# Mixture-of-experts layer: dense experts replaced by sorted rows, indirect transfers and a last summing pass

## Chip, cores, metric

One core of a Trainium2 chip runs the whole program. The metric is the device time of one launch in microseconds (us), median of several runs.

## What is computed

The input is `x`, 8 batches of 2048 rows of 256 numbers (16384 rows). First comes a landmark attention with 16 heads of 16 and 64 landmarks, with a residual and a layer norm; then a top-2 mixture of 8 experts, again with residual and layer norm:

```
x = layernorm(x + attention(x))
gate_logits = x @ Wg.T + bg                      # 8 experts
vals, idx   = top_k(gate_logits, 2)
gate_w      = softmax(vals)
all_out     = einsum('nd,ehd->neh', x, We) + be  # every expert, 256 x 256
out         = sum(all_out[idx] * gate_w)         # the two chosen ones
x = layernorm(x + out)
```

The kernel works in 32-bit floats. A product of full precision is made of three TensorE products with each factor split into a high and a low part (`product3`: high x high, low x high, high x low).

## The kernel before

A program for each engine is written out by hand; engines wait on semaphores, and instructions of one engine run in the order written. All plain transfers are issued by SyncE (SP), in one queue. The rows are cut into 32 chunks (`NCH`) of 512 (`CH`), four tiles (`TPC`) of 128 rows each.

Stage one (up to about 602 us) projects keys and values of all chunks, makes the landmark sums and inverts the landmark kernels. It is not touched, apart from the load of the experts' bias.

Stage two does, for each chunk: project queries (`queries`: TensorE L1618, ScalarE L805, VectorE `queries_lo` L1199); stack them by head with 16 transfers into the one buffer `q_stack` (`stack_queries_hi`, `stack_queries_lo`, `stack_query_norms`, L431 to L451); distances of eight head pairs (`query_dists`) and their exponentials into the one buffer `phi` (`q_exps`, L829) with a clamp on VectorE; `denominators` (L1663), their reciprocal, stored to memory and spread back over `attn` by two transfers (`store_inverses`, `spread_inverses`, L454, L462); `attention` and its scaling (`normalise`); split of the result (`attn_hi` on ScalarE L841, `attn_lo` on GpSimd L599); `output_projection` (L1688); `residual_stats` (VectorE L1254), `ln1` (GpSimd L615), `normalise_rows` (ScalarE L855); transposes of the rows, gate logits, their transpose, and the gates (`gates_begin`, `gates_end`).

Experts: `experts(p, n)` (L1749), 16 calls a chunk, each six products of 512 columns, so two experts for one tile of 128 rows; all eight experts are computed for every row. The results are weighed with the gate (zero for an expert not chosen): half of them on VectorE (`combine`, L1331), half on ScalarE (`weigh`, L891), whose parts GpSimd sums (`sum_parts`, L621). `finish`, `ln2` and `result` do the second layer norm, and the chunk is stored.

The loop `for p in range(NCH)` stands once in each engine's program (SP L528, GpSimd L641, ScalarE L941, VectorE L1393, TensorE L1794). In iteration p the experts work on chunk p, the first layer norm on c = p + 1, and the attention on q = p + 2 and q + 1. Two extracts give the order on ScalarE and TensorE: ScalarE runs `q_exps(q, 4..8)` with `weigh` between them, then `queries(q + 1)`, then `normalise_rows(c)`; TensorE runs `query_dists(q, 6..8)`, `experts`, `queries(q + 1)`, `denominators(q)`, and the 16 expert calls lie between all other steps.

Of the kernel before, what the change touches and what calls it, by code (L numbers as in the profile page):

```python
# [37 lines left out]
SLOTS = 32  # L38
PIVOTS = (3, 3, 3, 3, 3, 4, 4, 4, 4)


C_ID, C_HEAD, C_NEG, C_LO, C_M16, C_NSEL, C_IOTA, C_EXP, C_BES, C_EPS, C_MINUS, C_REG, C_END = (
    0, 128, 136, 200, 201, 217, 225, 233, 237, 238, 242, 246, 278)


def program(nc, xT, x, wq, wk, wv, wo, we, wg, bq, bk, bv, bo, be3, bg, temp, idx, gbase, consts, tri, out):
# [10 lines left out]
    xT_v = xT.rearrange("(k p) t -> p k t", p=P)  # L57
    x_v = x.rearrange("(c t p) d -> c p t d", t=TPC, p=P)
    out_v = out.rearrange("(c t p) d -> c p t d", t=TPC, p=P)

    ctx = ExitStack()
    with ctx:
# [3 lines left out]
        def sem(name):  # L66
            return ctx.enter_context(nc.semaphore(name))

# [36 lines left out]
        be_s = sb("be_s", [P, 2 * D], f32r)  # L105
# [11 lines left out]
        part_x = sb("part_x", [P, 2, KC, 2 * D])  # L117
# [4 lines left out]
        with nc.sbuf_tensor("augk0", [64, CH], f32r) as augk0, nc.sbuf_tensor("aug_hi", [32, CH], f32r) as aug_hi:  # L122
            augk = [augk0]
        y_spare = sb("y_spare", [P, TPC, D])
# [10 lines left out]
        st2, mv2, ve2, rs2, nm2 = (sb("st2", [P, TPC, 6]), sb("mv2", [P, TPC, 2]), sb("ve2", [P, TPC]),  # L135
                                   sb("rs2", [P, TPC]), sb("nm2", [P, TPC]))
        nt1, nt2 = sb("nt1", [P, TPC]), sb("nt2", [P, TPC])
        lg, m8, i8 = (sb("lg", [P, TPC, E]), sb("m8", [P, TPC, 8]),
                           sb("i8", [P, TPC, 8], u32))
        if2, gd, ge, gs, gw1, gw2 = (sb("if2", [P, TPC, 2]), sb("gd", [P, TPC]), sb("ge", [P, TPC]),  # L140
                                     sb("gs", [P, TPC]), sb("gw1", [P, TPC]), sb("gw2", [P, TPC]))
        oh1, oh2, gate, gate_h = (sb("oh1", [P, TPC, E]), sb("oh2", [P, TPC, E]),
                                  [sb(f"gate{i}", [P, TPC, E]) for i in range(2)],
                                  sb("gate_h", [P, TPC, E], f32r))
        g_st, g_t = sb("g_st", [P, TPC, 32]), sb("g_t", [P, P], f32r)
        logit_rows = sb("logit_rows", [P, P])


        with ExitStack() as stage1:
# [9 lines left out]
            with ExitStack() as setup:  # L159
                def sb0(name, shape, dt=f32):  # L160
                    return setup.enter_context(nc.sbuf_tensor(name, shape, dt))

                bdh = [sb0(f"bdh{i}", [P, KC, HPS, NL], f32r) for i in range(2)]
                bdl = [sb0(f"bdl{i}", [P, KC, HPS, NL], f32r) for i in range(2)]
                augm = [sb0(f"augm{i}", [64, KC, HPS, NL], f32r) for i in range(2)]
                be_raw, be_tmp = sb0("be_raw", [P, 2 * D]), sb0("be_tmp", [P, 2 * D], f32r)
# [5 lines left out]
        x_tok, y_out = sb("x_tok", [P, TPC, D]), [sb("y_out", [P, TPC, D]), y_spare]  # L172
        x1 = [sb(f"x1_{i}", [P, TPC, D]) for i in range(2)]
        x1h, x1l = [sb("x1h0", [P, KC, CH], f32r)], [sb("x1l0", [P, KC, CH], f32r)]
        x1h.append(sb("x1h1", [P, KC, CH], f32r))
        x1l.append(sb("x1l1", [P, KC, CH], f32r))
        parts = [[part_x[:, i, k] for k in range(KC)] for i in range(2)]
# [8 lines left out]
        we_raw = [a[:].rearrange("p t d -> p (t d)") for a in (*x1, *y_out)]  # L186
# [37 lines left out]
        wo_done, h_done, ln1_stats, ln1_coef, x1_ready, x1t_done, x1h_ready, x1l_ready = (  # L224
            sem("wo_done"), sem("h_done"), sem("ln1_stats"), sem("ln1_coef"), sem("x1_ready"),
            sem("x1t_done"), sem("x1h_ready"), sem("x1l_ready"))
        logits_done, logits_saved, gate_done, gate_read, gd_ready, ge_ready, gst_ready, gtr_done, gt_ready, be_done, be_added = (
            sem("logits_done"), sem("logits_saved"), sem("gate_done"), sem("gate_read"), sem("gd_ready"), sem("ge_ready"), sem("gst_ready"),
            sem("gtr_done"), sem("gt_ready"), sem("be_done"), sem("be_added"))
        ffn_done, comb_done, part_ready, part_sum, acc_done, ln2_stats, ln2_coef, res_ready, res_stored = (  # L230
            sem("ffn_done"), sem("comb_done"), sem("part_ready"), sem("part_sum"), sem("acc_done"), sem("ln2_stats"), sem("ln2_coef"),
            sem("res_ready"), [[sem(f"res_stored{i}{half}") for half in range(2)] for i in range(2)])
# [5 lines left out]

        def raw(ap):

            return ap.bitcast(f32)
# [37 lines left out]
        def expert_bank(p, n):  # L279

            return bank[(2, 3, 5)[(16 * p + n) % 3]]
# [26 lines left out]
        def _(sp):  # L308
# [3 lines left out]
            sp.sem_inc(acc_done, 2)  # L312
# [8 lines left out]
            for dst, src in ((cst, consts), (bq_sb, bq), (bk_sb, bk), (bv_sb, bv), (bo_sb, bo), (bg_sb, bg),  # L321
                             (temp_sb, temp), (be_raw, be3)):
# [163 lines left out]
            def store(p, half):  # L486

                sp.wait_ge(res_ready, TPC * p + 2 * half + 2)
                sp.dma_start(out_v[p, :, 2 * half:2 * half + 2],
                             y_out[p % 2][:, 2 * half:2 * half + 2]).then_inc(res_stored[p % 2][half], 16)  # L490
# [8 lines left out]
            for i in range(2 * KC):  # L499
# [1397 lines left out]
```

## Time and profile before

| | us |
|---|---|
| median of 3 runs | 2072.36 (2070.72 to 2078.35) |
| the profiled execution | 2077.58 |
| its span, first to last instruction | 2075.8 |

The busy time of each engine (us, share of the span, instructions), and the span in 40 equal slices, each digit the busy share in tenths; PEclk is TensorE's granted clock in tenths of full speed, DMA the mean busy share of the 16 DMA engines:

```profile
PE 1795.9 (87%) x18232; PEld 1363.1 (66%) x18232; DVE 1358.9 (65%) x3414; ACT 1141.1 (55%) x2171; POOL 753.2 (36%) x1113
...
PE   4578999999965699999989999899999899998987
...
PEclk9689999999986799999999999999999999999999
DMA  2686797778862444444553344443445434445310
```

PE is TensorE's products, PEld its weight loads, DVE VectorE, ACT ScalarE, POOL GpSimd, SPq the transfers that SP issues. A timeline row is start, length, engine, line, operation, output<-input and count; in brackets the idle time of the engine before it and what ended it. Products overlap: the distance between two starts says more than one's length.

### The profile page before, as it was taken

Reading aid. Unit: us, or ns where it says so; the run is one execution under the profiler, and the core shown is the slowest. Engines: PE = TensorE matmul, PEld = TensorE weight load, DVE = VectorE, ACT = ScalarE, POOL = GpSimd, SP = SyncE. Lnnn points to the kernel's source line nnn. Section 1 sums busy time; section 2 is a strip of 40 time slices with the busy share of each in tenths; the row PEclk is TensorE's granted clock in tenths of the full one; section 3 lists DMA queues with packets and bytes.
Section 4 is the critical chain, followed back from the end, with each engine's and each line's share of the span. In section 5 each row is a group of like instructions: output and inputs, shape, how many; then the busy total and the mean of one; then the engine's idle time right before and its main releaser. Section 6 shows DMA issues by size and latency. Waiting matters only on the chain. (4 is left out here: it accounts for less than half of the span.)

```text
span 2075.8 us, 46584 instructions
## 1 busy us (share of the span) xinstructions
PE 1795.9 (87%) x18232; PEld 1363.1 (66%) x18232; DVE 1358.9 (65%) x3414; ACT 1141.1 (55%) x2171; POOL 753.2 (36%) x1113
## 2 busy tenths in 40 slices
PE   4578999999965699999989999899999899998987
PEld 3167778778753466666666666666666666666666
DVE  5678845987334466776666766677766667666765
ACT  2256666667554365556556555555655654664533
POOL 2300000000002245555455554555555545545544
PEclk9689999999986799999999999999999999999999
DMA  2686797778862444444553344443445434445310
GB/s 84 97 169 145 168 189 169 166 164 185 162 184 73 90 109 107 93 92 92 114 114 87 88 99 109 110 102 89 93 98 116 107 83 93 93 108 112 77 38 26
DMA packets 223805, 233.38 MB, mean 112 GB/s; under 512 B 59873, under 2 KB 147297, under 8 KB 223329
## 3 DMA queue, kind: packets, MB, share of 16 engines
q1 hardware_dynamic: 223392, 229.87, 50.0%
q8 instruction: 144, 2.36, 0.5%
q14 instruction: 77, 0.62, 0.1%
q0 software_dynamic: 192, 0.52, 0.1%
HBM read 78.28 MB, written 25.69 MB: 50 GB/s over the span
## 5 line engine op out<-in xcount | busy, mean ns | idle before, releaser
L302 PE MATMUL bank<-weh,x1h 128*128 128x512 f32 x1024 | 441.5, 431 | 0.0
L304 PE MATMUL bank<-wel,x1h 128*128 128x512 f32 x1024 | 413.0, 403 | 0.0
L303 PE MATMUL bank<-weh,x1l 128*128 128x512 f32 x1024 | 412.4, 403 | 0.0
L897 ACT ACTIVATE part_x<-bank,gate 128x256 f32<-128x256 f32 x512 | 214.7, 471 | 285.9 <-PE bank L304 285.7
L838 ACT ACTIVATE phi<-bank,nlt,invt 128x512 f32<-128x512 f32 x256 | 185.2, 778 | 167.6 <-PE bank L1643 167.6
L302 PEld LDWEIGHTS bank<-weh,x1h 128*128 128x128 f32 x1024 | 199.5, 195 | 116.6 <-issue 77.1
L612 POOL TENSOR_TENSOR x_tok<-x_tok,bo_sb 128x512 f32<-128x512 f32 x64 | 81.5, 1299 | 529.7 <-DMA x_tok<-in_x 529.7
L625 POOL TENSOR_TENSOR part_x<-part_x 128x512 f32<-128x512 f32 x128 | 165.0, 1289 | 289.4 <-ACT part_x L897 289.4
L304 PEld LDWEIGHTS bank<-wel,x1h 128*128 128x128 f32 x1024 | 197.5, 193 | 48.1
L303 PEld LDWEIGHTS bank<-weh,x1l 128*128 128x128 f32 x1024 | 198.3, 194 | 35.3
L700 ACT ACTIVATE phi<-bank,invt 128x512 f32<-128x512 f32 x256 | 162.6, 684 | 106.6 <-PE bank L1532 106.3
L1531 PE MATMUL bank<-l_hh,k_hl 128*128 128x256 f32 x512 | 146.3, 317 | 39.8 <-DMA k_hl<-kh 29.0
L1068 DVE TENSOR_SCALAR phi<-phi,phi_max,phi_min 128x1024 f32<-128x1024 f32 x128 | 103.7, 810 | 106.0 <-ACT phi L700 105.8
L1252 DVE TENSOR_TENSOR attn<-bank,attn 128x512 f32<-128x512 f32 x64 | 43.8, 688 | 157.5 <-DMA attn<-den_dram 157.4
L1220 DVE TENSOR_SCALAR phi<-phi,phi_max,phi_min 128x1024 f32<-128x1024 f32 x128 | 131.2, 1026 | 17.0 <-ACT phi L838 16.8
L586 POOL TENSOR_TENSOR ve<-mv,cst 128x1 f32<-128x1 f32 (+1 forms) x160 | 46.2, 289 | 258.3 <-DVE mv L1355 157.9
L1531 PEld LDWEIGHTS bank<-l_hh,k_hl 128*128 128x128 f32 x512 | 100.6, 197 | 55.7 <-DMA k_hl<-kh 34.5
L1684 PE MATMUL bank<-phi,y_cur 128*32 128x512 f32 x512 | 72.1, 637 | 71.1 <-DVE attn L1252 71.1
L1532 PE MATMUL bank<-l_lo,k_ha 128*128 128x256 f32 x512 | 132.3, 289 | 0.0
L1643 PE MATMUL bank<-q_stack,l_stack 128*128 128x512 f32 x256 | 92.8, 445 | 45.6 <-DMA q_stack<-key_aug 34.8
L603 POOL TENSOR_TENSOR attn_l<-attn,attn_h 128x512 fp32r<-128x512 f32 x64 | 84.6, 1324 | 114.1 <-ACT attn_h L846 114.1
L302 PE MATMUL bank<-xh,wh 128*128 128x512 f32 x260 | 108.5, 417 | 13.3 <-DVE xl L1088 6.9
(200 smaller groups left out, 4111.1 us busy)
## 6 DMA issues: line engine op xcount, KB each, us to landing
x_raw<-in_xT SPq DMA_DIRECT2D x64, 512.0 KB, 5.1
q_stack<-kh SPq DMA_DIRECT2D x256, 128.0 KB, 2.4
x_tok<-in_x SPq DMA_DIRECT2D x32, 512.0 KB, 3.8
q_stack<-kl SPq DMA_DIRECT2D x128, 128.0 KB, 2.7
q_stack<-key_aug SPq DMA_DIRECT2D x128, 128.0 KB, 5.5
attn<-den_dram SPq DMA_DIRECT2D x64, 256.0 KB
k_hl<-attn_h SPq DMA_DIRECT2D x32, 256.0 KB, 4.7
k_ha<-attn_h SPq DMA_DIRECT2D x32, 256.0 KB, 5.1
```

The costliest lines, as they stand in the source:

```text
L302: nc.tensor.matmul(outp, ah, bh, start=first, stop=False)
L303: nc.tensor.matmul(outp, al, bh, start=False, stop=False)
L304: return nc.tensor.matmul(outp, ah, bl, start=False, stop=last)
L625: own.then(nc.gpsimd.tensor_tensor(a[0], a[0], a[1], ALU.add))
L700: nc.scalar.activation(phi[:, n], bank[6 + s][:], ACT.Exp, scale=invt[:]).then_inc(exp_done, 1)
L838: nc.scalar.activation(phi[:, i], bank[6 + i % 2][:], ACT.Exp, bias=nlt[:, c // CPB, i:i + 1], scale=invt[:]).then_inc(qexp_done, 1)
L897: last = nc.scalar.activation(parts[t % 2][n % 4 // 2][:, u * D:(u + 1) * D], expert_bank(p, n)[:, u * D:(u + 1) * D], ACT.Copy, scale=gat ...
L1068: V.tensor_scalar(tile, tile, phi_max[:], phi_min[:], ALU.min, ALU.max).then_inc(phi_ready, 1)
L1220: V.tensor_scalar(two, two, phi_max[:], phi_min[:], ALU.min, ALU.max).then_inc(qphi_ready, 2)
L1531: mm(dst, k_hl[at][:, g, tok], wide(hh), start=True, stop=False)
L1532: last = mm(dst, k_ha[at][:, g, tok], wide(lo), start=False, stop=True)
L1643: mm(bank[6 + i % 2][:], l_stack[c // CPB % 2][:, i].rearrange("p u k -> p (u k)"), q_stack[:, i], start=True, stop=True).then_inc(qdist_d ...
```

## The change

The experts leave the loop. After the gates of chunk p, VectorE finds each row's place in the region of its two experts (`find_places`, with ranks that TensorE counts by products in `ranks`), and GpSimd writes the chunk's rows there by eight indirect transfers of 128 rows of 260 numbers: the row, the two gates, its number, its first expert (`scatter`). Every fourth chunk VectorE plans which tiles of which expert are full (`plan`). After the loop there are 264 tiles of 128 rows: SP loads a tile from an address in a register, TensorE transposes it, ScalarE and VectorE split it, TensorE multiplies it with the expert whose number it loads into registers and adds the bias; ScalarE or VectorE weighs; GpSimd writes the terms back to each row's place by two indirect transfers for two tiles. The residual is part of the first expert's term (the identity is added to the weights). Then a last pass loads both terms of each chunk, adds, normalises and stores. The expert weights are loaded and split in iterations 1 to 5 of the loop and no longer ahead of it. The orders within an iteration change too.

```diff
+ROW = D + 4
+QUAD = 4
+ROWS_OF = (3, 7, 11, 15, 19, 23, 27, 31)
+TAKEN = (24, 32, 32, 32, 32, 32, 32, 32, 16)
+TILES = sum(TAKEN)
+IN_RING, OUT_RING, SUM_RING = 3, 4, 4
 ...
+            def load_tiles(n):
 ...
+                _, at = nc.values_load_multi_w_load_instructions(
+                    tile_row[0:1, QUAD * n:QUAD * (n + 1)], [mybir.EngineType.SP], ...)
+                for i in range(QUAD):
+                    sp.dma_start(tile_in[:, QUAD * ring + i], rows_dram[bass.ds(at[i], P), :]).then_inc(tile_loaded[ring], 16)
+            def load_terms(c):
+                ring = c % SUM_RING
+                if c >= SUM_RING:
+                    sp.wait_ge(res_stored[ring], 16 * (c // SUM_RING))
+                for u, dst in enumerate((term_a, term_b)):
+                    sp.dma_start(dst[ring], terms_v[u, c]).then_inc(sum_loaded[ring], 16)
+            def store(c):
+                sp.wait_ge(res_ready, TPC * (c + 1))
+                sp.dma_start(out_v[c], term_a[c % SUM_RING]).then_inc(res_stored[c % SUM_RING], 16)
 ...
@@ SP: the loop and what follows
-                if p:
-                    store(p - 1, 0)
                 load_rows(q)
+                store_inverses(q)
                 stack_queries_hi(q + 1)
-                store_inverses(q)
                 stack_queries_lo(q + 1)
                 spread_inverses(q)
                 stack_query_norms(q + 1)
-                if p:
-                    store(p - 1, 1)
                 load_query_x(q + 3)
+                load_weights(p)
+            for n in range(TILES // QUAD):
+                load_tiles(n)
+            for i in range(OUT_RING):
+                sp.wait_ge(term_stored[i], 32 * len(range(i, TILES // 2, OUT_RING)))
+            for c in range(SUM_RING):
+                load_terms(c)
+            for c in range(NCH):
+                store(c)
+                if c + SUM_RING < NCH:
+                    load_terms(c + SUM_RING)
@@ GpSimd: the loop and what follows
                 ln1(c)
-                sum_parts(p, 0)
                 residual(q)
-                ln2(p, 0)
-                sum_parts(p, 1)
+                scatter(p)
                 split_lo(q + 2, 1)
                 attn_lo(q, 0)
-                ln2(p, 1)
-                sum_parts(p, 2)
                 attn_lo(q, 1)
+            scatter_pads()
+            for m in range(TILES // 2):
+                scatter_terms(m)
+            for c in range(NCH):
+                ln2(c)
@@ ScalarE: the loop, as it is after
+                q_exps(q, range(4, 6))
+                x1_copy(p)
+                q_exps(q, range(6, 8))
+                normalise_rows(c, c % 2)
+                save_logits(p)
+                queries(q + 1)
+                gate_exp(p)
+                query_hi(q + 2, 1)
+                if begins_batch(q + 1):
+                    for g in (1, 2):
+                        landmarks_of_batch((q + 1) // CPB, g)
+                q_exps(q + 1, range(0, 2))
+                attn_hi(q, 0)
+                attn_hi(q, 1)
+                if begins_batch(q + 2):
+                    landmarks_of_batch((q + 2) // CPB, 0)
+                q_exps(q + 1, range(2, 4))
+                weights_hi(p)
@@ VectorE: the loop, as it is after
+                q_clamp(q, range(4, 6))
+                residual_stats(c, c % 2)
+                q_clamp(q, range(6, 8))
+                gates_begin(p)
+                invert_denominators(q)
+                queries_lo(q + 1)
+                gates_end(p)
+                find_places(p)
+                query_norms(q + 1)
+                normalise(q, 0)
+                normalise(q, 1)
+                weights_lo(p)
+                q_clamp(q + 1, range(0, 4))
+                if p in ROWS_OF:
+                    plan(ROWS_OF.index(p))
@@ TensorE: the loop and what follows, as they are after
+                x1_transposes(p)
+                query_dists(q, range(4, 6))
+                output_projection(c)
+                gate_logits(p)
+                query_dists(q, range(6, 8))
+                logit_transpose(p)
+                denominators(q)
+                queries(q + 1, 1)
+                attention(q, 0)
+                ranks(p)
+                query_norms(q + 1)
+                attention(q, 1)
+                query_dists(q + 1, range(0, 4))
+                if begins_batch(q + 1):
+                    z_transposes((q + 1) // CPB)
+                    landmark_solve((q + 1) // CPB)
+            tile_transposes(0)
+            for m in range(TILES // 2):
+                if m % 2 == 0:
+                    numbers = experts_of_quad(m // 2)
+                if m + 1 < TILES // 2:
+                    tile_transposes(m + 1)
+                expert(m, numbers)
```

`expert(m, ...)` does two tiles, each six products of 256 columns and one for the bias. `scatter(p)` waits for `find_places(p)`, and `residual_stats(c)` for the scatters of chunk c - 2.

## Rows read from the trace of the kernel before

**Rows 1.** Stretches: length, engines' busy us (count), granted clock, DMA share, GB/s

```profile
602.00:624.00 22.00, 6.37 (x65) 4.67 (x65) 3.95 (x8) 12.05 (x31) 2.52 (x2) 0.69 0.87 227
684.00:700.00 16.00, 0.74 (x9) 0.50 (x2) 1.83 (x4) 1.51 (x3) 2.51 (x2) 0.55 1.01 173
1100.00:1200.00 100.00, 92.81 (x675) 69.22 (x677) 70.81 (x204) 57.61 (x117) 53.61 (x83) 0.98 0.40 92
```

**Rows 2.** Costliest group of the page: operation, count, busy us and mean ns, idle before

```profile
L302 PE MATMUL bank<-weh,x1h 128*128 128x512 f32 x1024 | 441.5, 431 | 0.0
```

**Rows 3.** Timeline of the transfer queue and ScalarE: start us, us, operation

```profile
680.90 5.97 SPq L428 DMA_DIRECT2D q_stack<-kh  x8
...
1946.73 5.10 SPq L428 DMA_DIRECT2D q_stack<-kh  x8
1990.44 0.60 SPq L460 DMA_DIRECT2D den_dram<-den_inv  x1
...
2002.17 0.63 ACT L846 ACTIVATE attn_h<-attn 128x512 fp32r<-128x512 f32 x1 [2.84 <-DVE attn L1252]
```

**Rows 4.** Timeline of the fill, each link of a chunk's chain on its engine

```profile
623.95 1.22 PE L1643 MATMUL bank<-q_stack,l_stack 128*128 128x512 f32 x2 [12.98 <-DMA q_stack<-key_aug]
624.79 1.45 ACT L838 ACTIVATE phi<-bank,nlt,invt 128x512 f32<-128x512 f32 x2 [6.38 <-PE bank L1643]
...
662.37 0.58 PE L302 MATMUL bank<-wh,attn_h 128*128 128x256 f32 x1 [1.69 <-POOL attn_l L603]
...
667.90 0.76 DVE L1261 TENSOR_TENSOR x<-bank,x_tok 128x256 f32<-128x256 f32 x2 [1.07 <-PE bank L304]
...
672.09 3.55 PE L1672 MATMUL bank<-phi,y_cur 128*32 128x128 f32 x64 [4.23 <-DVE phi L1220]
673.55 2.08 ACT L860 ACTIVATE x<-x,nm,rs 128x256 f32<-128x256 f32 x4 [12.06 <-POOL nm L589]
675.58 0.50 PE L302 MATMUL bank<-xh,wh 128*128 128x512 f32 x1
...
679.26 0.68 ACT L814 ACTIVATE sq<-bank,bq_sb 128x512 f32<-128x512 f32 x1
...
688.22 1.23 ACT L846 ACTIVATE attn_h<-attn 128x512 fp32r<-128x512 f32 x2 [3.70 <-DVE attn L1252]
688.93 2.51 POOL L603 TENSOR_TENSOR attn_l<-attn,attn_h 128x512 fp32r<-128x512 f32 x2 [5.46 <-ACT attn_h L846]
...
699.43 0.80 PE L1643 MATMUL bank<-q_stack,l_stack 128*128 128x512 f32 x1 [15.26 <-DMA q_stack<-key_aug]
```

**Rows 5.** Timeline of TensorE in the loop, at the full clock

```profile
1281.08 0.39 PE L302 MATMUL bank<-weh,x1h 128*128 128x512 f32 x1
1281.31 0.39 PE L303 MATMUL bank<-weh,x1l 128*128 128x512 f32 x1
...
1294.92 1.03 PE L1712 MATMUL bank<-cst,x 128*128 128x128 f32 x8
...
1322.96 0.28 PE L303 MATMUL bank<-wh,attn_l 128*128 128x256 f32 x1
1323.08 0.29 PE L304 MATMUL bank<-wl,attn_h 128*128 128x256 f32 x1
...
1331.85 1.95 PE L1672 MATMUL bank<-phi,y_cur 128*32 128x128 f32 x64
```

**Rows 6.** Timeline of GpSimd's indirect gathers, and their time to landing

```profile
5.52 0.95 POOL L559 DMA_INDIRECT phi<-in_x,rows_sb  x1 [0.30 <-issue]
6.78 0.95 POOL L559 DMA_INDIRECT phi<-in_x,rows_sb  x1 [0.31 <-issue]
...
DMA to landing us min/median/max: 3.8/4.8/6.7
```

**Rows 7.** Transfers by line: count, KB each, median us to landing

```profile
out<-y_out SPq DMA_DIRECT2D x32, 256.0 KB, 3.0
idx_sb<-in_idx SPq DMA_DIRECT2D x1, 0.5 KB, 1.9
```

More of the change, by code:

```diff
@@ L134, in program @@
                                    sb("rs1", [P, TPC]), sb("nm1", [P, TPC]))
[L135 to L146, printed above, removed]
+        nt1 = sb("nt1", [P, TPC])
         with ExitStack() as stage1:
@@ L227, in program @@
[L227 to L232, printed above, removed]
+            sem("x1t_done"), sem("x1c_ready"))
@@ L277, in begins_batch, with tile_batch @@
             return c % CPB == 0 and not past_end(c)
-        def expert_bank(p, n):
-            return bank[(2, 3, 5)[(16 * p + n) % 3]]
+        def tile_batch(n):
+            return next(s for s in range(len(TAKEN)) if n < sum(TAKEN[:s + 1]))
         def pairs_of(a, j, u=slice(None)):
@@ L1424, in _ @@
                     landmark_values((q + 1) // CPB)
-            finish(NCH - 1, 3)
+            pads()
+            plan(len(ROWS_OF))
+            pick(0)
+            tile_lo(0)
+            for m in range(TILES // 2):
+                if m % 2 == 0 and m // 2 + 1 < TILES // QUAD:
+                    pick(m // 2 + 1)
+                if m + 1 < TILES // 2:
+                    tile_lo(m + 1)
+                if m % 2 == 0:
+                    weigh(m)
+            for c in range(NCH):
+                sum_terms(c)
@@ L1720, in gate_logits @@
                 for k in range(KC):
[L1721 to L1724 removed]
+                    for t in range(TPC):
+                        last = mm(bank[2][32 * t:32 * t + 32, 0:P], wg_s[:, k], x1_T[:, k, t * P:(t + 1) * P],
+                                  start=(k == 0), stop=(k == KC - 1))
@@ new lines, in experts_of_quad, with expert @@
+            def experts_of_quad(n):
+                return nc.values_load_multi_w_load_instructions(
+                    tile_ei[0:1, QUAD * n:QUAD * (n + 1)], [mybir.EngineType.PE], min_val=0, max_val=E - 1,
+                    skip_runtime_bounds_check_because="an expert's number is a position among the eight")[1]
+            def expert(m, numbers):
+                pe.wait_ge(xt_l_ready, m + 1)
+                if m >= 2:
+                    pe.wait_ge(term_ready[m % 2], m // 2)
+                for i in range(2):
+                    dst, cols = bank[m % 2][:, i * D:(i + 1) * D], bass.ds(numbers[2 * (m % 2) + i] * D, D)
+                    for k in range(KC):
+                        at = slice((2 * i + k) * P, (2 * i + k + 1) * P)
+                        product3(dst, xt_h[m % 2][:, at], xt_l[m % 2][:, at], weh[:, k, cols], wel[:, k, cols], k == 0, False)
+                    last = mm(dst, ones32[:], be_s[:, cols], start=False, stop=True)
```

644 lines of the change are left out of this document (348 added, 296 removed).

## The prediction

> **What bounds the kernel now.** I read the stretches of the run first. TensorE is busy 93% of a hundred microseconds in the second stage at a granted clock of 0.98, while the DMA engines are at 0.40 [rows 1]; the costliest group is the experts' product with all eight experts, 1024 instructions for each of its three factors [rows 2]. A 512-column product starts 0.234 us after the one before, a 256-column one 0.12 us [rows 5]; so a chunk's 96 expert products hold TensorE 22.4 us. The loop over chunks is timed by the start of a chunk's first query-stacking transfer: 680.90 for chunk 2, 1946.73 for chunk 31, 29 chunks, 43.65 us each [rows 3]. The run is then stage one (to 602), a fill of some 100 us, 29 periods (1266 us), and an end of 110. The fill is where to look next: there the experts don't run yet, and each step of a chunk stands bare in time [rows 4].
>
> **What the change does to that.** It takes the expert products out of the loop and puts two serial phases behind it: 264 tiles through their expert, then a pass that loads both terms of each row, adds, normalises and stores. Expert work falls from 3072 products of 512 columns (3072 x 0.234 = 719 us) to 264 x 7 of 256 (1848 x 0.12 = 222 us). The gain can only come from a shorter loop period, so that is the first thing to work out.
>
> **The loop.** The instructions per chunk that stay are well below the period: TensorE 43.65 - 22.4 at most. What decides is the order. In the new ScalarE order `normalise_rows(c)` and `save_logits(p)` stand ahead of `queries(q+1)`, and on TensorE `logit_transpose(p)` and `denominators(q)` stand ahead of `queries(q+1)`. Before, the queries stood ahead of all of these. `output_projection(c)` needs `attn_hi(c)`, which now stands behind `q_exps(q, 0:2)`, and these need the queries of q stacked. So from "chunk q stacked" to "chunk q+1 stacked" there is one chain, and it is the period. Its links, each as the fill shows it [rows 4]: products and exponentials of two pairs, 623.95 to 626.24, 2.3; attention rows split high and low, 688.22 to 691.44, 3.2; output projection, 662.37 to 667.90, 5.5; residual, statistics and POOL's coefficients, 667.90 to 673.55, 5.65; normalising four tiles, 2.1; saving and transposing the logits, 0.6 (an estimate from a 128 x 128 copy's and a transpose's size); denominators, 3.55; queries from the first product to the last square, 675.58 to 679.94, 4.4; stacking, from the first transfer's issue to the first product that uses it, 680.90 to 699.43, 18.5 [rows 3, 4]. Sum 45.8: no link can start before the last one ends.
>
> Two bounds on it. The output projection and the denominators ran at the half clock in the fill, after the idle wait for stacking; at full clock they take 24 x 0.12 = 2.9 and 1.95 [rows 5], and the chain is 41.6. The granted clock was 0.55 while TensorE waited for the stacking and 0.69 in the stretch of 602 to 624 [rows 1]; the new loop has the same wait each chunk, so I take the half clock. Upwards: eight scatters of 128 rows a chunk (1.06 MB) run beside the stacking, because `find_places(p)` ends some 4 us after the queries. The DMA share was 1.01 at 173 GB/s there already [rows 1]; at the 227 GB/s of share 0.87 that is 1.06/0.261 = 4.1 us more at worst, and nothing at best, as the fill's stacking had 0.75 MB of other loads (query rows, inverse) issued behind it within the same stretch. I take nothing, and 4 for the range. Once in four chunks the landmark copies (2.8 us), the landmark solve (about 3) and the plan of tiles (some 20 small VectorE steps, 7 us, of which 4 stay uncovered by the output projection) fall into the chain: (2.8 + 3 + 4)/4 = 2.4. The period is then 45.8 + 2.4 = 48.2; I use 48, bounds 41.6 and 52. What stays hidden: POOL's eight scatter issues at 1.25 us each [rows 6], 10 us between the places and the next `attn_lo`, with about 3 us to spare (at 1.6 us each they would end too late); VectorE's gate work, beside ScalarE's queries and the stacking.
>
> **The start and the end of the loop.** Stage one is unchanged. In the fill the expert weights' load and split are gone; the residual there waited for the projection anyway, so only the stretched low split and some DMA time return, 3 us: chunk 2 is stacked at 699.4 - 3 = 696. Chunk 31 is stacked at 696 + 29 x 48 = 2088. From there: the chain up to the denominators once more, 2.3 + 3.2 + 5.5 + 5.65 + 2.1 + 0.6 + 3.55 = 22.9; reciprocal 1.3; store and spread of the inverses to the split, 1990.44 to 2002.17, 11.7 [rows 3]; split, projection, residual and normalising of chunk 31, 2.5 + 5.5 + 5.65 + 2.1 = 15.8; transposes, logits, gates and places about 8.5; the last plan 7. TensorE can begin on tiles 67 us after, at 2155. POOL issues chunk 31's eight scatters and eight of pads first: 60 + 20 = 80 us after.
>
> **The tile phase.** Per four tiles: TensorE 28 x 0.12 + 8 transposes in 1.03 [rows 5] = 4.4 us at full clock; POOL four scatters at 1.25 = 5.0 [rows 6]; DMA 1.06 MB, 4.1 us at the 261 GB/s above, 6.1 at 173. To these comes what no row shows: four loads of an expert's number into TensorE's registers, with TensorE waiting. Bounds: POOL's gap of 0.3 us between two issues [rows 6], where another engine hides it all, and the 1.9 us of the smallest transfer [rows 7] twice over. I take 1.4, nearer to the first, so 5.8 per four, 66 x 5.8 = 383 us; bounds 66 x 5.0 = 330 and, with a clock that stays at half (28 x 0.23 + 2 = 8.4, plus the loads), 66 x 9 = 594. One page has a price for the loads: the Trainium skill, DMA: Bandwidth & Descriptors, section Latency and other measured facts, gives about 600 ns as the floor of a tensor load. By an estimate from it, four in series would be 2.4 us, and the phase 66 x 6.8 = 449 us; no row here shows it. With 3 to fill the pipe and 5 for the last terms to land (indirect transfers landed in 3.8 to 6.7 us [rows 6]) the phase ends at 2155 + 391 = 2546.
>
> **The sum pass.** In SP's order `load_terms(c+4)` waits until the store of chunk c has landed, and `store(c+1)` is issued behind it. So each chunk costs the issue of two loads and a store, and the time of 1.57 MB to pass, in order, on one queue: at 261 GB/s 6.0, and about 1 of landing: 7.0 us; bounds 5 (a 256 KB store landed 3.0 after its issue [rows 7], and about 2 go to issuing) and 9 (at 173 GB/s). The engines are below that: residual, statistics and coefficients of such a chunk were 5.65 over two engines, normalising 2.1 [rows 4]. First store 13 us in, 28 x 7.0 = 196, four without loads 13, landing 4: 226 us. The same page's fit in Anatomy of one DMA (2.0 us and bytes over 436 GB/s) would by an estimate make 5.6 of a chunk, 40 us less in all; the highest rate that a stretch here shows is lower, and I go by that.
>
> **Sum.** 696 + 1392 + 67 + 391 + 226 = 2772 us of span; the profiled run took 2077.6 for a span of 2075.8, so 2774, **2775 us**. That profiled execution lies 5 us above the median of the three (2072.4), far below what is uncertain here. The kernel gets slower by a third: 497 us of TensorE's products go, but the loop was never 22 us from its next bound.
>
> **Rivals.**
> *The chain at full clock.* If TensorE keeps 2.4 GHz, period 41.6 and tiles at 5.0: 2775 - 29 x 6.4 - 53 = 2536. For it: the loop of before, with short gaps, held 0.98 [rows 1]. Against it: a wait of more than 10 us every chunk.
> *Tiles slower.* Register loads in series with a half clock, 9 us per four: 2775 + 211 = 2986. For it: it is the one price without a row.
> *The chain is shorter.* If stacking needs only its bytes at the highest rate (2.6 MB with the spread, at 261 GB/s 10 us, and 3 of landing), 5.5 us go from the chain: period 42.7, and 38.5 with the full clock too: 2620 or, with the tiles at 5.0 as well, 2447. For it: issue and landing could overlap better in a quiet queue. Against it: the one bare case took 18.5.
> *The other side: the loop falls to what the DMA engines need.* Per chunk 3.6 MB of today's 4.1 and 1.06 of scatters, 4.7 MB; at 227 GB/s 20.6 us, and if the chain runs over several chunks at once the period would be about 22: 2775 - 29 x 26 = 2021, faster by 3%. It decides below a period of (2077.6 - 696 - 67 - 391 - 226 - 1.8)/29 = 24.0 us. `q_stack`, `phi` and `attn` have one buffer each and the orders are fixed, which speaks against it.
> *It does not cut the work.* 264 tiles are always run, a quarter of the rows times experts and 3% more; I see no case in which it would run all.
>
> **Chances.** Forecast (2600 to 2950) 0.58; full clock 0.16; shorter chain 0.10; tiles slower 0.11; other side 0.03, a mixture near no change 0.02. A measurement of this kernel can tell about 0.5% from no change. Faster by over 0.5% 0.03, within 0.01, slower 0.96. The range takes in the full clock, half of the shorter chain and most of the slower tiles: 2450 to 2970.
>
> **What would show it.** In the changed kernel: stacking transfers 46 to 50 us apart in the loop, TensorE half idle with a granted clock well under 0.98; ScalarE's `kh` of the next chunk only after `x1` is normalised; a tile phase of 390 us with POOL and TensorE both near full; a last pass of 226 with the DMA engines as the only busy part. Wrong, if the stacking starts come under 40 us apart, if indirect issues take over 1.6 us each, or if SP does not wait for stores in the last pass.

## The result, and the profile after

The changed kernel takes 2849.16 us (median of 4 runs, 2844.34 to 2861.72) against 2071.54 (2069.52 to 2078.35) before: ratio 1.3755, 95% interval 1.3701 to 1.381. 2775 was forecast. The profiled execution has a span of 2847.8 us. Below, a time without a range comes from a single execution.

From the page of the changed kernel: engines' busy time, the 40 slices of TensorE, its granted clock and the DMA share, and the lines of the chain that ended last:

```profile
PE 1644.8 (58%) x17248; PEld 1247.9 (44%) x17248; DVE 1222.0 (43%) x3392; ACT 1045.6 (37%) x1891; POOL 901.1 (32%) x1001
...
PE   5589989974444454454544445445354699997000
...
PEclk8799999986666666566665666666666799999555
DMA  2868676844343433424334243342424366665666
...
DMA q_stack<-key_aug 8%; SPq L463 8%; PE bank L338 7%; DMA out<-phi 6%; PE bank L339 6%; PE bank L340 6%; PE bank L1826 4%; ACT phi L942 3%; PE bank L1921 2%; PE bank L1901 2%; SPq L486 2%; PE bank L1797 2%; PE bank L1685 2%; ACT x L964 2%; SPq L505 2%
```

Slices 10 to 30 are the loop: TensorE four to five tenths busy, at a clock of 0.6 where it held 0.98 [rows 1]. Then come five slices of tiles, TensorE full at full clock, and three of the sum pass, in which TensorE does nothing. The same in stretches (columns as in [rows 1]; loop, tiles, sum pass):

```profile
700.00:1500.00 800.00, 378.99 (x2931) 260.99 (x2929) 268.28 (x943) 251.01 (x467) 274.33 (x283) 0.64 0.38 100
2250.00:2550.00 300.00, 300.00 (x1916) 244.50 (x1915) 145.58 (x429) 101.92 (x212) 205.38 (x215) 1.00 0.61 189
2650.00:2810.00 160.00, 0.00 (x0) 0.00 (x0) 67.52 (x200) 47.68 (x92) 35.29 (x88) 0.50 0.70 222
```

The first stacking transfers of chunks 2 and 31 in the timeline of the queue, which give the period as [rows 3] did:

```profile
679.11 5.24 SPq L463 DMA_DIRECT2D q_stack<-kh  x8
...
2143.60 5.41 SPq L463 DMA_DIRECT2D q_stack<-kh  x8
```

29 periods of 50.50 us, against 43.65. So the parts of the span stand against the forecast like this (us):

| | forecast | trace |
|---|---|---|
| chunk 2 stacked (first product on it) | 696 | 696.6 |
| loop, chunk 2 stacked to chunk 31 stacked | 29 x 48 = 1392 | 2162.0 - 696.6 = 1465.4 |
| chunk 31 stacked to the first tile's transpose | 67 | 79.0 |
| tile phase, to the first load of the sum pass | 391 | 381.5 |
| sum pass | 226 | 225.3 |
| span | 2772 | 2847.8 |

The loop alone accounts for 73 of the 76 us missed, and the start of the tiles for 12; the tiles give back 10.

### The profile page after: what moved, and what is told of

Its sections match the earlier page's. It is cut to its first block, busy times and chain, and to the rows that moved or that the text cites. A ratio compares the mean times of both kernels' runs of the same rounds, so it can differ in the third digit from the quotient of the medians.

```text
span 2847.8 us, 46793 instructions
## 1 busy us (share of the span) xinstructions
PE 1644.8 (58%) x17248; PEld 1247.9 (44%) x17248; DVE 1222.0 (43%) x3392; ACT 1045.6 (37%) x1891; POOL 901.1 (32%) x1001
## 4 chain that ended last, share of the span: by engine, by line
PE 38%; DMA 17%; SPq 15%; DVE 10%; ACT 9%; issue 6%; POOL 5%; ACTq 0%; POOLq 0%; DVEq 0%
DMA q_stack<-key_aug 8%; SPq L463 8%; PE bank L338 7%; DMA out<-phi 6%; PE bank L339 6%; PE bank L340 6%; PE bank L1826 4%; ACT phi L942 3%; PE bank L1921 2%; PE bank L1901 2%; SPq L486 2%; PE bank L1797 2%; PE bank L1685 2%; ACT x L964 2%; SPq L505 2%
## 5 line engine op out<-in xcount | busy, mean ns | idle before, releaser
L711 POOL DMA_INDIRECT rows_dram<-x,place_i x256 | 248.3, 970 | 421.6 <-DVE place_i L1414 352.9
L1838 PE MATMUL bank<-phi,y_cur 128*32 128x512 f32 x512 | 93.8, 816 | 476.3 <-DVE attn L1349 476.3
L1349 DVE TENSOR_TENSOR attn<-bank,attn 128x512 f32<-128x512 f32 x64 | 44.1, 691 | 480.4 <-DMA attn<-den_dram 416.3
L1838 PEld LDWEIGHTS bank<-phi,y_cur 128*32 128x32 f32 x512 | 12.7, 123 | 495.4 <-issue 495.4
L1797 PE MATMUL bank<-q_stack,l_stack 128*128 128x512 f32 x256 | 150.2, 668 | 90.0 <-DMA q_stack<-key_aug 55.5
L338 PE MATMUL bank<-weh,q_stack 128*128 x528 | 174.5, 331 | 0.6 <-DVE q_stack L1485 0.6
L1485 DVE TENSOR_TENSOR q_stack<-bank,q_stack 128x512 fp32r<-128x512 f32 x132 | 91.3, 692 | 137.5 <-ACT q_stack L1008 137.5
L339 PE MATMUL bank<-weh,q_stack 128*128 x528 | 148.5, 281 | 0.0
L340 PE MATMUL bank<-wel,q_stack 128*128 x528 | 148.1, 280 | 0.0
L1797 PEld LDWEIGHTS bank<-q_stack,l_stack 128*128 128x128 f32 x256 | 62.0, 273 | 192.3 <-DMA q_stack<-key_aug 107.3
L730 POOL DMA_INDIRECT terms_dram<-attn,tile_to x132 | 126.6, 959 | 58.3 <-issue 20.4
L730 POOL DMA_INDIRECT terms_dram<-x_T,tile_to x132 | 126.6, 959 | 58.1 <-issue 20.4
L338 PE MATMUL bank<-wh,attn_h 128*128 128x256 f32 x256 | 97.6, 381 | 68.4 <-ACT x_T L974 66.3
L1008 ACT ACTIVATE q_stack<-bank 128x512 fp32r<-128x512 f32 x132 | 78.9, 598 | 157.1 <-PE bank L1901 157.1
```

Source lines behind the costliest of these rows:

```text
L338: nc.tensor.matmul(outp, ah, bh, start=first, stop=False)
L339: nc.tensor.matmul(outp, al, bh, start=False, stop=False)
L340: return nc.tensor.matmul(outp, ah, bl, start=False, stop=last)
L711: nc.gpsimd.indirect_dma_start(out=rows_dram, out_offset=bass.IndirectOffsetOnAxis(ap=place_i[:, at:at + 1].bitcast(u32), axis=0), in_=x1[ ...
L730: nc.gpsimd.indirect_dma_start(out=terms_dram, out_offset=bass.IndirectOffsetOnAxis(ap=tile_to[:, at:at + 1].bitcast(u32), axis=0), in_=te ...
L1797: mm(bank[6 + i % 2][:], l_stack[c // CPB % 2][:, i].rearrange("p u k -> p (u k)"), q_stack[:, i], start=True, stop=True).then_inc(qdist_d ...
```

## Experiments

Periods below are all read as above: the first stacking transfer of chunk 31 less that of chunk 2, over 29. "The change" is the changed kernel as it was measured above.

**The first look: the copy, and SyncE's wait in the sum pass.** TensorE's waits between 750 and 2000 us of the changed kernel (who waits, for whom: us in all, times, longest) hold one that my chain did not have, the last of these three:

```profile
PE bank L1838 <- DVE attn L1349: 387.9, 24, 18.8
PE bank L1797 <- DMA q_stack<-key_aug: 18.7, 22, 1.6
PE bank L338 <- ACT x_T L974: 55.5, 25, 3.5
```

L338 is the output projection, L974 is `x1_copy`. The first line says something else too: the long wait of each chunk, 16.2 us, ends for TensorE with the inverses of the denominators (L1838 is the second half of attention, L1349 its scaling), and behind that half TensorE waits another 0.85 us for the stacking (L1797 is the distances). Both go through SyncE's one queue, the spread of the inverses in the middle of the stacking, and they end nearly together. The waits of SyncE's queue in the sum pass (2640 to 2840 us):

```profile
SPq L565 <- DMA out<-phi: 152.5, 27, 6.1
```

```diff
-                q_exps(q, range(4, 6))
                 x1_copy(p)
+                q_exps(q, range(4, 6))
                 q_exps(q, range(6, 8))
@@ SP, sum pass
-                if c + SUM_RING < NCH:
-                    load_terms(c + SUM_RING)
+                if c and c - 1 + SUM_RING < NCH:
+                    load_terms(c - 1 + SUM_RING)
```

> Two edits, one in the loop and one in the sum pass, read apart in the trace. (a) ScalarE copies the first-layer rows of chunk p (x1_copy) ahead of q_exps(q, 4..6) and no longer behind. Theory, the copy is a missed link of the chain (output_projection waits for it through the bank that it frees, 2.2 us of TensorE's wait a chunk): the loop's period falls from 50.5 to about 48.4 us. Rival, the wait for the copy only covers another one that ends as late (the split rows of attention): the period stays within 0.5 us of 50.5. (b) In the sum pass SyncE issues the loads of a chunk one step later, so that the store they wait for has had a whole chunk's time to land. Theory, the pass is bound by the landing of the store just issued: 7.08 us per chunk falls to about 6.1. Rival, the DMA engines' rate is the bound: it stays at 7.0 or more. Both theories right: 2849 - 29 x 2.1 - 28 x 0.9 = about 2763 us in all.

2735.3 us. Period 48.22, 2.28 less. The wait is all but gone, in the same stretch:

```profile
PE bank L338 <- ACT x_T L974: 6.5, 9, 2.2
```

The sum pass takes 170.6 us in place of 225.3; its stores come 5.08 us apart (2582.74 to 2714.91, 26 steps), not the 6.1 expected, and the DMA engines are full, at a rate above all that the trace of before showed (2590 to 2640 us, columns as above):

```profile
2590.00:2640.00 50.00, 0.00 (x0) 0.00 (x0) 30.13 (x90) 20.74 (x40) 20.03 (x41) 0.50 0.97 314
```

So the wait for the store just issued was the bound (the DMA share was 0.70 with it), and the next one is the engines' rate, at 314 GB/s and not at 261.

**Queries first, and 128 rows in the bias product.**

```diff
@@ ScalarE
+                queries(q + 1)
                 normalise_rows(c, c % 2)
                 save_logits(p)
-                queries(q + 1)
@@ TensorE
-                logit_transpose(p)
+                queries(q + 1, 1)
                 denominators(q)
-                queries(q + 1, 1)
+                logit_transpose(p)
@@ VectorE: queries_lo, then invert_denominators, gates; SP: stack_queries_hi, then store_inverses
@@ buffers
-    be_s [32, E * D], ones32 [32, P]
+    be_s [P, E * D] (rows 32 to 127 zero), ones32 [P, P]
```

> Two edits, one in the loop and one in the tile phase. (a) The order of before for the queries: on all engines queries(q + 1) and the stacking of its high halves come ahead of the normalising, the logits and the denominators. Theory of the one chain: residual, statistics, coefficients, normalising, logits and denominators (5.65 + 2.1 + 0.6 + 3.1 us) leave the path from one stacking to the next as far as they are not needed, and the period falls from 50.5 to about 40 to 42 us. Rival, the stacking with its scatters and the inverses' way to memory and back is a chain of its own that ends as late: the period falls by less than 3 us. (b) The tiles' bias product takes 128 rows (96 of them zeros) and no longer 32. Theory, the change of the product's row count costs 0.3 to 0.4 us per tile: four tiles take 5.0 to 5.2 us (GpSimd's four indirect issues at 1.25 become the bound) instead of 5.62. Rival, the time behind the bias product is the wait for the next tile's split rows or the expert's registers: 5.6 stays. Both theories right: 2849 - 29 x 9 - 66 x 0.5 = about 2555 us; both rivals: above 2760.

2501.5 us; period 39.51, 11.0 less, a little more than expected: the one chain is borne out, and the order alone makes a fifth of the period. And the tiles come at 5.06 us per four, over all 264. Their timeline on TensorE, with 32 rows in the bias product (L1921) as the change has it,

```profile
2404.66 0.37 PE L338 MATMUL bank<-weh,q_stack 128*128 x1
...
2405.34 0.28 PE L340 MATMUL bank<-wel,q_stack 128*128 x1
2405.55 0.38 PE L1921 MATMUL bank<-be_s,ones 32*128 x1
2405.86 0.38 PE L338 MATMUL bank<-weh,q_stack 128*128 x1
```

and with 128:

```profile
2056.15 0.28 PE L338 MATMUL bank<-weh,q_stack 128*128 x1
...
2056.73 0.28 PE L340 MATMUL bank<-wel,q_stack 128*128 x1
2056.85 0.28 PE L1922 MATMUL bank<-be_s,ones 128*128 x1
2056.97 0.49 PE L1902 MATMUL bank<-cst,tile_in 128*128 128x128 f32 x3
```

Seven products take 1.20 us in the first and 0.82 in the second (0.92 for a tile that follows transposes, as the one shown in the first does). In the second GpSimd is next: its indirect issues lie 1.26 us apart, four of them 5.04.

**A busy TensorE for the clock, in two steps.** First 96 products that nobody reads, in the wait for the stacking:

```diff
                 query_norms(q + 1)
+                for _ in range(96): mm(bank[2][:, 256:512], wh.., wh.., start=True, stop=True)
                 attention(q, 1)
```

> In each iteration TensorE does 96 products of 256 columns whose result nobody reads, in its 15.6 us wait for the stacking. They cost no path time (11.5 us at full clock). Theory, the half clock that follows the wait costs the chain the difference between its rows at either level (output projection, denominators, attention: 5.5 to 2.9, 3.06 to 1.95, 1.94 to 1.06): granted clock in the loop from 0.64 to over 0.9, the period from 50.5 down to 46 to 47.5 us, the run to about 2740. Rival, the chain's links are bound by ScalarE and VectorE between the products, and the clock matters little: the period falls by less than 1.5 us though the clock rises. Second rival, the clock is granted by something other than recent work: it stays at 0.64 to 0.75.

2871 us, period 51.08: 0.6 more, where the theory expected 3 to 4.5 less. The test was not a fair one. The granted clock of the loop rose (0.77 of 700 to 2050 us, from 0.64), but not where the chain needs it. One iteration in stretches: the last of the dummies ends at 1464.2, and the chain goes on at 1468:

```profile
1458.00:1464.00 6.00, 6.00 (x52) 5.99 (x50) 0.00 (x0) 0.00 (x0) 4.62 (x5) 1.00 0.87 252
1464.00:1468.00 4.00, 0.30 (x6) 0.13 (x8) 0.69 (x1) 0.00 (x0) 2.66 (x3) 0.95 0.85 211
1468.00:1471.00 3.00, 1.83 (x8) 0.10 (x7) 0.69 (x1) 0.00 (x0) 0.00 (x0) 0.50 0.88 195
```

So the second step, dummies up to the end of this wait and of the one for the logits:

```diff
+                pe.wait_ge(qphi_ready, PAIRS * (q + 1))
+                for _ in range(24): mm(bank[7][:, 256:512], ...)
                 logit_transpose(p)
                 denominators(q)
 ...
-                for _ in range(96): ...
+                for _ in range(124): ...
                 attention(q, 1)
```

> The change as it is, with dummy products of 256 columns up to the end of both waits: 124 in the wait for the stacking (14.6 us of 15.6, up to about 1 us ahead of attention's second half) and 24 in the 6 us wait for the logits. In the run before, with 96, the granted clock was 1.00 during the dummies and 0.50 again 4 us after their end, so that the links of the chain still ran at the half clock. Theory, the chain pays for the half clock: now attention takes 1.06 and no longer 1.94, denominators 1.95 and no longer 3.1, the period falls by 2 to 3.5 us, to 47 to 48.5. Rival, the clock costs the chain little, since ScalarE and VectorE set the pace between the products: the period stays at 50 to 51 although these rows are at full clock.

2803.4 us, period 48.71: 1.8 less, with 0.87 in 700 to 2050. Now attention and denominators are rows of the full clock (1.06 and 1.95 us):

```profile
1823.65 1.06 PE L1838 MATMUL bank<-phi,y_cur 128*32 128x512 f32 x8 [1.88 <-DVE attn L1349]
...
1844.43 1.95 PE L1826 MATMUL bank<-phi,y_cur 128*32 128x128 f32 x64
```

But not the output projection. The denominators' products (L1826) and a third of the projection's (L339) between 750 and 2050 us, in the change and then here; behind the bar stand busy us and mean ns of one:

```profile
L1826 PE MATMUL bank<-phi,y_cur 128*32 128x128 f32 x1664 | 91.5, 411 | 0.0
L339 PE MATMUL bank<-wh,attn_l 128*128 128x256 f32 x208 | 76.2, 366 | 0.0
```
```profile
L1826 PE MATMUL bank<-phi,y_cur 128*32 128x128 f32 x1728 | 53.1, 275 | 0.0
L339 PE MATMUL bank<-wh,attn_l 128*128 128x256 f32 x216 | 79.4, 368 | 0.0
```

From the denominators to the queries the chain takes 1.90 us where it took 3.45 (means over 29 chunks); the output projection takes 4.5, as it did (4.6), and the 3.0 of the full clock in a few chunks only. The saving of 1.8 in the period, just short of the 2 to 3.5 expected, is thus the denominators' saving, nearly whole. What the full clock would give in the projection, by an estimate from these rows up to 1.6 us more, no run here shows. The first step's extra 0.6 lies for the most part between the first stacking transfer and the first product (20.7 us in the mean, 20.2 in the change); what lengthens it stays open.

**Scatters beside the stacking.**

```diff
-    out=rows_dram, in_=x1[p % 2][:, t]
+    out=rows_dram viewed as four pieces of 65 columns, index 4 * place + 3, in_=x1[p % 2][:, t, 195:ROW]
```

(The second line is in words; the tile loads read the same 65 columns. The number of transfers and rows stays, three quarters of the bytes go.)

> The scatters in the loop write the last 65 of 260 columns of each row (260 bytes), to the same rows, and the tile loads read these columns alone; the other columns of a tile are left over from earlier, so the experts' output is left wrong. The number of descriptors and of issues on GpSimd stays, three quarters of the scatters' bytes go. Theory of the prediction, scatters beside the stacking cost nothing: from the first stacking transfer to the first product that uses it stays 19.9 us, the period 50.5. Rival, the DMA engines' bytes are the bound there (share 0.88, 235 GB/s): 0.8 MB less is up to 3.1 us off the stacking, the period 47.5 to 49. Second rival, the descriptors and not the bytes take the time: stacking unchanged too, with the DMA share unchanged at 0.8 or more and the rate down. The tile phase is not the question here.

2815.6 us. Period 49.20, 1.3 less; from the first stacking transfer to the first product 18.6 us in the mean of 29 chunks (20.2 with whole rows). In 13 us of the stacking (1541 to 1554 of the change, 1522 to 1535 here) the DMA share is 0.78 at 187 GB/s, from 0.87 at 232. So bytes count: three quarters of them cost 1.3 us a chunk, a little less than the 1.5 to 3 the rival expected and not the nothing that I took. What the last quarter and the number of rows cost is not shown.

**All four edits, then the queries still earlier.**

> The four edits of the first two runs together: queries ahead of normalising, logits and denominators; the copy of the first-layer rows ahead of the exponentials; 128 rows in the bias product; loads of the sum pass issued one step later. Theory, these are separate links and separate phases and add up: period 39.5 - 2.2 = 37.3 us, tiles 5.09 per four, sum pass 5.1 per chunk, run 2501 - 64 - 54 = about 2383 us. Rival, with the queries early the copy's wait is covered by the exponentials: period 39.0 or more, run 2430 or more.

2362.1 us (2360.2 to 2365.1), ratio to before 1.1377 (1.1324 to 1.143); period 36.91. They add up: 50.50 - 11.0 - 2.3 would be 37.2.

```diff
@@ TensorE, from the four edits
                 x1_transposes(p)
-                query_dists(q, range(4, 6))
-                output_projection(c)
+                query_dists(q, range(4, 8))
                 gate_logits(p)
-                query_dists(q, range(6, 8))
                 queries(q + 1, 1)
                 denominators(q)
+                query_norms(q + 1)
                 logit_transpose(p)
+                output_projection(c)
+                ranks(p)
                 attention(q, 0)
-                ranks(p)
-                query_norms(q + 1)
@@ ScalarE, VectorE accordingly; GpSimd: scatter ahead of residual
@@ SP: hi, lo and norms stacked, then store_inverses, spread_inverses, load_rows
```

> As the run before, and now the last two pairs' distances, the queries of the next chunk and the denominators come ahead of the output projection of the chunk before on all engines; the norms are stacked ahead of the inverses' way to memory. What is left between two stackings is distances and exponentials of eight pairs (about 7 us with the split rows between them), the queries (4.4) and the stacking (18.7). Theory, the one chain is only as long as its links: period 30 to 33 us, run about 2383 - 29 x 5.5 = 2220 us, still above the kernel before, since the break-even period is 24.0 us. Rival, the way of the inverses (denominators, reciprocal, store, spread behind the stacking, attention's second half, exponentials 4 to 8) becomes the chain: period 35 to 37, run 2320 to 2380.

2429.8 us, ratio 1.1714 (1.1659 to 1.1769): period 39.40, longer than with the four edits, and longer than the rival gave. TensorE's waits between 750 and 1650 us:

```profile
PE bank L1837 <- DVE attn L1348: 339.9, 23, 17.9
```

14.8 us a chunk for the inverses, which SyncE now issues last. Their place alone was changed next: stored behind the high halves, spread ahead of the norms.

> As the run with the queries ahead of the output projection, which went from 36.9 to 39.4 us a period, with one difference on SyncE: the inverses are stored and spread ahead of the norms' stacking, as they are with the four edits, and no longer behind it. In the run before, the spread landed 20 us after the first stacking transfer's issue and TensorE's second half of attention, and the distances behind it, waited for it (14.8 us of wait a chunk; first stacking transfer to first distance 23.2 us against 18.7). Theory, the way of the inverses through the one queue is the bound, and its place in that queue costs the difference: first transfer to first distance back to 18.5 to 20, period 34 to 36, run 2270 to 2335 us. Rival, the wait for the inverses is as long wherever they stand: period 39 or more, run 2415 or more.

2325.6 us, ratio 1.1196 (1.1154 to 1.1239); period 35.34, as the theory had it; the same wait, in the same stretch:

```profile
PE bank L1837 <- DVE attn L1348: 232.6, 25, 11.5
```

The place of the inverses' two steps in one queue was 4.1 us of every period. This is the fastest version here that scatters rows, and it is 12% slower than the kernel before: its period is 11 us above the 24.0 at which the change would break even as it stands, and with its own, shorter end (613.2 us from chunk 31's first stacking transfer) the break-even is still only (2075.8 - 680.3 - 613.2)/29 = 27.0.

**The kernel before, with fewer expert products.** Would a lighter TensorE have brought anything at all in the old loop? With one product of six, and the weighing and summing on the other engines left as they were:

```diff
-    for k in range(KC):
-        last = product3(expert_bank(p, n)[:], x1h.., x1l.., weh.., wel.., k == 0, k == KC - 1)
+    last = nc.tensor.matmul(expert_bank(p, n)[:], x1h[at][:, 0, tok], weh[:, 0, cols], start=True, stop=True)
```

> The kernel before, with one product of six in each expert call (TensorE's 96 products of 512 columns a chunk become 16; high by high parts of the first half of the channels alone), all else of the loop as it was, so the output is not the layer's. 80 x 0.234 = 18.7 us of TensorE's work a chunk go. Theory, the loop before was near its next bound (VectorE busy 31 us of a period, the chain of stacking and queries some 32 to 36): the period falls from 43.65 by 6 to 12 us only, to 32 to 37, the run to 1735 to 1890. Rival, TensorE was the bound by far and the rest would follow: the period falls by nearly all of 18.7, to 25 to 27, the run to about 1550, and moving the products behind the loop had been worth its price in itself.

2024.8 us: both expectations missed. Period 42.14, only 1.5 less, for 18.7 us of TensorE's work taken away. With `product3` of the first half of the channels kept (three of six):

> The kernel before with three of six products in each expert call (the second half of the channels left out), so the output is not the layer's: 48 x 0.234 = 11.2 us of TensorE's work a chunk go, where 18.7 went in the run with one product. That run gained 1.5 us a period (43.65 to 42.14) and its granted clock in the loop was 0.71. Theory A, the chain through stacking, inverses and VectorE's order is as long as the period at any clock: 42 us here as well, a little either way, and the rest of TensorE's 11 us becomes waiting. Theory B, the chain is shorter at full clock and was stretched by the half clock in that run: here, with TensorE busier and the clock higher, the period falls to 38 to 40, below that of the run with fewer products. Rival, TensorE's work is the bound down to some 32 us: the period falls by nearly 11 us.

2017.9 us, period 41.87. Theory A. Before, one product and three products, 1100 to 1900 us of each:

```profile
1100.00:1900.00 800.00, 731.23 (x5275) 536.43 (x5274) 544.86 (x1587) 450.94 (x918) 415.17 (x624) 0.97 0.45 99
```
```profile
1100.00:1900.00 800.00, 532.20 (x3870) 341.11 (x3871) 559.94 (x1627) 446.77 (x936) 422.51 (x637) 0.70 0.46 101
```
```profile
1100.00:1900.00 800.00, 601.10 (x4679) 409.83 (x4671) 558.21 (x1655) 463.53 (x962) 434.94 (x653) 0.88 0.47 104
```

TensorE at 0.70, 0.88 and 0.97 of its clock, 67 to 91% busy, and the same 42 to 43.65 us. What the loop waits for instead stands in its timeline with one product: VectorE, in order, waits for the spread inverses, ScalarE and TensorE wait for VectorE, and GpSimd for ScalarE:

```profile
1752.34 0.69 DVE L1252 TENSOR_TENSOR attn<-bank,attn 128x512 f32<-128x512 f32 x1 [8.60 <-DMA attn<-den_dram]
1752.95 0.41 DVE L1351 TENSOR_TENSOR y_out<-y_out,part_x 128x256 f32<-128x256 f32 x1
1753.07 0.63 ACT L846 ACTIVATE attn_h<-attn 128x512 fp32r<-128x512 f32 x1 [7.06 <-DVE attn L1252]
1753.18 1.94 PE L1684 MATMUL bank<-phi,y_cur 128*32 128x512 f32 x8 [7.41 <-DVE attn L1252]
```

Over the same 800 us this wait of VectorE grew from the first line (the kernel before) to the second (one product):

```profile
DVE attn L1252 <- DMA attn<-den_dram: 85.2, 18, 5.7
```
```profile
DVE attn L1252 <- DMA attn<-den_dram: 143.0, 19, 9.0
```

The weighing and summing stayed in both runs (VectorE 70% busy), so what the old order would do without them too was not tried.

## Why the prediction was right, point by point

**The bound.** "The loop was never 22 us from its next bound" holds more sharply than I knew: with the other engines' expert work in place it was 1.8 us from it. TensorE 93% busy was no evidence of a gain; the expert products filled waits that were there anyway. Removing the products alone leaves 42. The change makes it 50.5, and the order is the greatest part of that: with the queries put first again, ahead of normalising, logits and denominators, 11.0 of it go.

**The period, 48 against 50.5.** The chain is right, and its links can be read one by one in the timelines of the changed kernel (us, means over the 29 chunks):

| | forecast | trace |
|---|---|---|
| first stacking transfer to the first product on it | 18.5 | 20.2 |
| that product to the output projection | 2.3 + 3.2 = 5.5 | 9.6 |
| output projection to the start of normalising | 5.5 + 5.65 = 11.15 | 9.8 |
| normalising and logits, to the denominators | 2.1 + 0.6 = 2.7 | 2.7 |
| denominators to the queries | 3.55 | 3.45 |
| queries to the first stacking transfer | 4.4 | 4.8 |
| once in four chunks: landmarks and plan | 2.4 | in the rows above |
| sum | 48.2 | 50.5 |

The step that failed is in the second row, a missing link: "`output_projection(c)` needs `attn_hi(c)`" is true, but it also needs the banks that `x1_copy(p)` empties, and ScalarE does that behind two more groups of exponentials. I had read that copy as long done. In chunks without landmark work this row is 7.9 us, and 5.8 with the copy moved ahead; moving it took 2.3 from the period. The landmark copies make it 10.2 and the landmark solve 12.1, each once in four chunks, 1.6 us a chunk where I had (2.8 + 3)/4. The plan, for which I had another 1.0 a chunk, shows in no row of the change: in its chunks the second row is 7.9 and the start of normalising no later. The second miss is a term's size: the scatters beside the stacking, taken at 0 with a bound of 4, are the 1.7 of the first row (18.6 with a quarter of their bytes), and measured 1.3 in the period. Against these stands the third row, 1.35 too long: I had the projection at the half clock throughout, 5.5 us to the residual, and it takes 4.6 to its end.

**The clock.** Half clock in the loop was right in the mean (0.64), and so was its cause, a long wait each chunk. Its price is shown in part. For the denominators I had 3.55 less 1.95, 1.6 us, and holding the clock there gave 1.55. For the output projection I had 5.5 less 2.9, and it was 4.6 to begin with; the full clock was not held there in any run. And the rival's own sum was wrong: its period of 41.6 leaves out the 2.4 for landmarks and plan, which the 48 has. With them it is 44.0, and the rival's total 2775 - 29 x 4 - 53 = 2606 in place of 2536.

**The end of the loop, 67 against 79.** Chunk 31's places stand 68.6 us after its stacking, 60 forecast: its transposes start 3.7 us late (55.4 against 51.7), and from there to the places are 13.1 us, not 8.5, 2.7 of them a wait of the one `place_i` for chunk 30's scatters to land. And there are two plans, chunk 31's and the spare tiles', 10.1 us together; I had counted one at 7.

**The tiles.** 5.62 us per four against 5.8, right for the wrong reason. The 1.4 that I added for register loads is not in the trace: in the steady phase no wait of TensorE lies beside them, so another engine or TensorE's own products hide them. The time is in the bias product's 32 rows between products of 128, 0.36 to 0.38 a tile, which the trace of before could not show. The Trainium skill's figure in DMA: Bandwidth & Descriptors, section Latency and other measured facts (about 600 ns for a tensor load), had by the estimate made the phase 449 us; the trace, with 381.5, does not bear out four of them in series. What one such load takes no run here shows.

**The sum pass.** 225.3 us of 226, 7.13 per chunk (stores at 2640.10 to 2832.52, 27 steps), and the mechanism, SyncE's wait for the store just issued, is shown by moving it. The 261 GB/s that I held for the highest rate is not one: without the wait the rate is 314 and a chunk takes 5.08. The Trainium skill, DMA: Bandwidth & Descriptors, section Anatomy of one DMA, gives 2.0 us and bytes over 436 GB/s for one transfer issued by GpSimd; I had used it for three issued by SyncE. By that estimate a chunk takes 5.6 us; the pass as written took 7.13 and the one with the later loads 5.08, so the estimate fits neither closely.

**Rivals.** A shorter chain had the stacking at 13 us; it took 20.2 in the change and 18.6 with a quarter of the scatters' bytes. Slower tiles had the half clock, and the phase held 1.00. The other side, a loop bound by the DMA engines at 22 us, is far: with all that was moved here, the loop stays at 35.3 us, of which 9.3 (232.6/25) is TensorE's wait for the inverses.

**Luck.** 2775 against 2849 is nearer than the parts: the tiles' 10 us, the 1.35 us a chunk of the third row (39 us in 29 chunks) and the plan's 1.0 hid a part of what the missing link and the scatters cost.

## What to carry over

Before work is taken off the busiest engine, take it off in a throwaway version and look at the period: here 18.7 us less work gave 1.5, and one such run prices the hoped-for gain. List the links of a loop's chain from the waits in the code, those for a bank or buffer to come free too, not only those for data. In an order written by hand, look first at the place of the step that starts the longest transfer, and of each transfer in its queue: here they were worth 11.0 and 4.1 us of a period, and 80 products of 512 columns removed 1.5.

## What the runs showed of the hardware

A product over 32 rows between products over 128 rows cost time on both sides: 0.21 us from the start before to its own and 0.31 from its own to the next, where 0.12 is usual; filled up with zeros to 128 rows, it starts and ends at 0.12. The granted clock went from 1.00 to 0.50 between the stretches 1458 to 1464 and 1468 to 1471 us when TensorE went idle for 3.7 us after 21.9 us of work without a gap, the last 11.8 of them dummy products. And loads and stores of 512 KB on one queue ran at 314 GB/s with a DMA share of 0.97, where the stacking of small pieces had filled the engines at 173 [rows 1].
